# Late fetch of weights, fillers on TensorE, and half the pauses between row scatters in a hybrid layer kernel

## What is computed

```python
x = x + attn_a(_layernorm(x), Wq, Wk, Wv, Wo, bo, q_norm_w, k_norm_w)
x = x + ffn(_layernorm(x), gate_weight, Wg, Wu, Wd, Sg, Su, Sd)
x = x + attn_b(_layernorm(x), Wa, Wx, ba, bx, Lam)
x = x + ffn(_layernorm(x), gate_weight, Wg, Wu, Wd, Sg, Su, Sd)
```

## Time and profile before

| | |
|---|---|
| median of 3 runs | 1233.53 us (1233.43 to 1235.91) |
| the profiled execution | 1236.23 us, its span 1234.1 us |
| busy in the span | PE 997.5 us (81%), ACT 739.3 (60%), DVE 520.1 (42%), POOL 410.5 (33%) |
| mean granted clock of TensorE | 0.90 of 2.4 GHz |
| chain that ended last | PE 29% of the span, POOL 11%, issue 4%, DMA 3%, DVE 3% |

### The profile page before, as it was taken

How to read it: one execution, slowest core, us unless ns; L and a number is a source line. 1 busy time by engine, 2 the same in 40 slices (tenths; PEclk the granted TensorE clock), 3 DMA queues, 4 the chain that set the end, 5 groups by cost and what they waited for, 6 DMA issues and landing times.

```text
span 1234.1 us, 20310 instructions
## 1 busy us (share of the span) xinstructions
PE 997.5 (81%) x7268; PEld 644.7 (52%) x7268; DVE 520.1 (42%) x1575; ACT 739.3 (60%) x982; POOL 410.5 (33%) x404
## 2 busy tenths in 40 slices
PE   5888777886898788977638999944887774999978
PEld 3543232331345446444328999922454434999966
DVE  7772711454212333521332333348875741333325
ACT  3588899999999999999103444414453400444430
POOL 0000000000230025055143556610388884566550
PEclk9999888989998999999678999956888976999987
DMA  9992000000110002000498999548132524999948
GB/s 352 394 392 78 1 1 1 18 2 11 49 50 23 18 33 90 2 21 4 142 264 234 292 289 290 109 151 271 50 121 109 160 66 125 268 290 279 268 63 330
DMA packets 94948, 176.21 MB, mean 143 GB/s; under 512 B 13134, under 2 KB 46895, under 8 KB 94848
## 3 DMA queue, kind: packets, MB, share of 16 engines
q1 hardware_dynamic: 57744, 129.86, 31.5%
q0 software_dynamic: 23616, 28.44, 10.9%
q10 hardware_dynamic: 13488, 16.62, 4.9%
HBM read 107.30 MB, written 83.72 MB: 155 GB/s over the span
## 4 chain that ended last, share of the span: by engine, by line
PE 29%; POOL 11%; issue 4%; DMA 3%; DVE 3%; DVEq 1%; ACT 0%; POOLq 0%; SPq 0%; ACTq 0%
PE PS L1459 14%; PE PS L1470 9%; POOL expert_in L335 8%; POOL pause L343 3%; PE PS L1446 2%; PE PS L1515 1%; DMA XE<-expert_in 1%; PE PS L1499 1%; DMA spare_space<-expert_out 1%; DMA expert_in<-xp,didx 1%; PE PS L1548 1%; DMA expert_out<-ob,yidx 1%; PE PS L1389 0%; PE PS L1404 0%; POOL expert_out L1345 0%
## 5 line engine op out<-in xcount | busy, mean ns | idle before, releaser
L335 POOL DMA_INDIRECT expert_in<-xp,didx x192 | 193.6, 1008 | 618.2 <-ACT PR L779 496.6
L774 ACT ACTIVATE PR<-PS 128x1024 f32<-128x1024 f32 (+3 forms) x312 | 276.5, 960 | 30.8 <-PE PS L643 15.2
L779 ACT ACTIVATE PR<-PR 128x2048 f32<-128x2048 f32 (+3 forms) x156 | 274.1, 1759 | 0.0
L1345 POOL DMA_INDIRECT expert_out<-ob,yidx x128 | 180.6, 1411 | 157.4 <-ACT ob L1657 117.5
L663 PE MATMUL PS<-PR,V 128*32 128x512 f32 (+3 forms) x768 | 94.9, 568 | 43.4 <-ACT PR L779 43.4
L1906 DVE SCALAR_TENSOR_TENSOR gta<-gth,PS 88x192 f32<-88x192 f32 x128 | 44.8, 350 | 192.8 <-ACT gth L1647 192.8
L643 PE MATMUL PS<-QT,KT 96*128 96x512 bf16 (+3 forms) x384 | 103.7, 363 | 12.4 <-ACT PR L774 9.8
L1647 ACT ACTIVATE gth<-PS 88x192 f32<-88x192 f32 x128 | 41.8, 326 | 106.6 <-PE PS L1459 106.6
L1657 ACT ACTIVATE ob<-PS,wslot 96x256 f32<-96x256 f32 x128 | 60.1, 469 | 62.1 <-PE PS L1470 59.9
L1459 PEld LDWEIGHTS PS<-XT,spare_space 128*88 128x88 f32 x960 | 91.7, 163 | 8.8 <-issue 2.6
L668 PE MATMUL PS<-PR,V 128*32 128x256 f32 x960 | 66.8, 392 | 34.9 <-ACT PR L779 34.6
(11 more groups left out here) (271 smaller groups left out, 1552.6 us busy)
## 6 DMA issues: line engine op xcount, KB each, us to landing
spare_space<-in_wgu SPq DMA_DIRECT2D x60, 352.0 KB
expert_out<-zero SPq DMA_DIRECT2D x2, 8256.0 KB, 50.5
expert_in<-zero SPq DMA_DIRECT2D x2, 7776.0 KB, 39.4
XE<-expert_in ACTq DMA_DIRECT2D x32, 486.0 KB
WGU<-in_wgu SPq DMA_DIRECT2D x44, 352.0 KB
spare_space<-expert_out SPq DMA_DIRECT2D x24, 512.0 KB, 6.2
spare_space<-in_wd SPq DMA_DIRECT2D x60, 176.0 KB
shared_space<-in_wgu SPq DMA_DIRECT2D x24, 352.0 KB
```

Of the source, the lines that this page charges most:

```text
L335: pool.indirect_dma_start(out=buf_d[f], out_offset=bass.IndirectOffsetOnAxis(ap=didx[b][:, r, j:j + 1], axis=0), in_=xp[b][:, r, :], in_of ...
L774: act.activation(PR[:, n % 3, 2 * pr:2 * pr + 2, cols(v, s):CW], PS[:, S0 + 2 * pr:S0 + 2 * pr + 2, cols(v, s):CW], ACT.Tanh, scale=1.0 / ...
L779: act.activation(PR[:, n % 3, :, lo:CW], PR[:, n % 3, :, lo:CW], ACT.Exp, scale=SOFT_CAP).then_inc(exp_done, 1)
L1345: pool.indirect_dma_start(out=y_d[f], out_offset=bass.IndirectOffsetOnAxis(ap=yidx[:, n % 4, j:j + 1], axis=0), in_=ob[:, i % EU, :], in_o ...
```

## The change

On GpSimd the pause follows every second row scatter instead of each. On SP the weights of experts 10 to 13 and wab are issued after the first XE has landed, wab behind them. On TensorE `fill(n)` issues n matmuls of 128x256 whose result, in bank 7, nobody reads; it stands at eleven places around the expert passes and between them, and in combine_late the wait on out_copied moves ahead of the one on O95, with 15 fillers between them. Before the fillers that follow the first pass a wait on out_copied is added.

```diff
-                    if pause is not None:
-                        n = CT * TOPK * (k - NC) + r * TOPK + j
+                    if pause is not None and j % 2:
+                        n = (CT * TOPK * (k - NC) + r * TOPK + j) // 2
                         if n:
                             pool.wait_ge(paused, n)
                         pool.memset(pause[:], 0.0).then_inc(paused, 1)
...
             first_spare(0)
+            sp.wait_ge(x_ld[0], 16)
+            first_spare2(0)
             sp.dma_start(wab[:], wab_d).then_inc(wab_loaded, 16)
-            first_spare2(0)
             experts(0)
...
+            def fill(n, bank=V0):
+                for _ in range(n):
+                    pe.matmul(PS[:, bank, 0:2 * P], const("ident"), consts[:, 0:2 * P], start=True, stop=True, skip_group_check=True)
...
             def combine_late():
                 pe.wait_ge(xt_ready, NH * 2)
+                pe.wait_ge(out_copied, 2 * E)
+                fill(15)
                 pe.wait_ge(o95_loaded, 32)
-                pe.wait_ge(out_copied, 2 * E)
...
             shared_down(K0)
+            fill(14)
             experts(0)
+            pe.wait_ge(out_copied, E)
+            fill(12)
             overflow_rows(0)
+            fill(4)
             overflow_rows(1)
+            fill(13)
             turn_recur(0)
             for c in range(NC + 1):
                 k = NC + c - 1
                 if c:
+                    fill(8 if c == 1 else 2)
                     turn_rows(k)
                     logits(k)
                 if c < NC:
                     gates(c)
+                if c == 0:
+                    fill(12)
                 if c:
                     place(k)
...
                 if c < NC:
+                    fill(8 if c == 0 else 2)
                     turn_state(c)
...
             shared_down(NC + K0)
+            fill(14)
             experts(1)
             combine_late()
```

## The result

The changed kernel takes 1220.36 us in the median (1218.26 to 1224.97), the kernel before on the same chip 1234.72 (1233.43 to 1236.26): a ratio of 0.9892, with a 95% interval of 0.9861 to 0.9922. The profiled execution took 1218.63 us, its span 1216.4. The prediction was 1215.5, between 1206 and 1226. On one of the chips that the experiments used, the very same kernel was not faster at all (1.0022). That is the second result of this study. The experiments show where the time goes there, and leave open which path inside the chip is held up.

A forecast was written before the change was run, and what follows sets the result against it. Passes are TensorE-bound; gains lie around them, in XE's wait, VectorE's and GpSimd's routing, and the end. 6.0 + 0 + 8.3 + 2.7 + 1.0 = 18.0 less than 1236.23 gives 1218.2; 2.7 lower for the median, 1215.5; range 1206 to 1226.

The forecast's parts named there:

- Part 1: In front of the first pass: weights issued behind XE let it load in 4.18 instead of 10.40 us; 6.0 us won.
- the rival's 3.7: In front of the first pass: older weights have a tail, so 3.7 us won; with a cold second start 1221, chance 0.17.
- The rule of the Trainium skill: DMA engines alternate between queues packet by packet; by turns alone XE takes 5.2 us, making the sum 1.0 us smaller.
- Part 2 and 3: Filler price 0.48 us warm, 0.93 cold; fillers around the first pass and in routing, 0 before the pass, 0.9 at turn_state.
- The slower rival: Fillers behind gates(0) run cold and delay the overflow matmuls; 9.1 us slower, 1243 us, chance 0.06.
- Part 4: Middle-stage scatters: 36 pauses fewer, then routing takes over the chain from GpSimd; 8.3 us won, bounds 5.5 and 11.3.
- denser scatters hold other engines: Rival in the middle-stage scatters: VectorE's small operations wait for scatter pairs, so 6.7 us lost there; 1230.5 us, chance 0.05.
- Part 5: Second expert pass: 14 fillers leave a 0.9 us gap before XE, so it starts warm; 2.7 us won, cold 0.
- shared_down ends at 1025.65 less 1.8: Before the second pass: step placing the 14 fillers at 1023.9 to 1030.6, with XE at 1031.5.
- Part 6: The end: 15 fillers speed the overflow matmuls, VectorE then sets the end; 1.0 us taken, between 1.7 won and 0.6 later.
- The likeliest case: The whole kernel: the forecaster's own case, 1210 to 1220 us, chance 0.55.
- the rival with a tail and a cold start: Older weights slow XE before the first pass and the second pass starts cold; 1221 us, chance 0.17.

The follow-up runs named there:

- ring_late: Changed kernel with the weights of experts 14 to 21 also issued behind the first XE: 1235.27 us, ratio 0.9996, on the chip where the unchanged changed kernel took 1237.03.
- fill_only: Kernel before with the fillers alone and their two waits on out_copied: 1232.68 us, ratio 1.0001.
- pause_only: Kernel before with half the pauses alone: 1223.36 us, ratio 0.9918.
- no_fill: Changed kernel with fillers of length zero, leaving late fetch and half pauses: 1223.63 us, ratio 0.9908.
- late_only: Kernel before with the late fetch alone: 1230.34 us, ratio 0.9979.
- after_again: The changed kernel, unchanged, measured again on another chip against the kernel before: 1237.03 us, ratio 1.0022.
- long_fill: Changed kernel with 32 and 28 fillers in place of 14 before the first and second expert pass: 1238.61 us, ratio 1.0042.
- the first comparison: The study's main measurement, the changed kernel against the kernel before on the same chip: 1220.36 against 1234.72 us, ratio 0.9892.
- pair_pause: Changed kernel with a second, short memset and its wait behind the pause after every second scatter: 1239.36 us, ratio 1.0049.
- three_quarters: Changed kernel with a pause left out behind every fourth scatter only: 1226.38 us, ratio 0.9942.
- no_pause: Changed kernel with no pauses at all between scatters: 1274.71 us, ratio 1.0306.

## Why the prediction was right in its number, and where not

**Part 1, the late fetch: the mechanism right, the size wrong.** I took 6.0 "because the volume says so" and 3.6 us were found. The mis-sized term is the end of the older weights: reckoned from the mean rate of the stretch they were through at 638, and ring_late shows that they are what still slows XE (6.47 with them, 4.44 without) and the last scatter (6.30 and 1.92, on the same chip). The row that spoke for a tail, wab's 16.9 us, was the better witness: the rival's 3.7 is next to what was measured. The rule of the Trainium skill that I had weighed against the step (DMA: Bandwidth & Descriptors, "Queues, rings and completion order": the engines take turns between queues) made it 5.2 us for XE with the new weights gone; measured are 6.00 to 8.55. The trace agrees with the rule in that a queue of weights slows XE without blocking it. Neither the rule nor my volume counted the older weights.

No clear wait of the pass on the late weights came up: 155.34 us, and 154.9 to 156.2 in the eight other first passes that have this late fetch and began cold, against 155.1 to 155.4 in the three without it. The pass has room for four late experts, and ring_late shows that it has none for twelve.

**Part 2 and 3, fillers.** Prices (0.44 us each warm, where I had 0.48) and covers hold. The 12 behind gates(0) ran warm, 5.34 us for 24 records, and the overflow matmuls behind them ended at 838.52, half a microsecond before VectorE's addition at 839.08, which came without a wait. The slower rival, cold fillers at this place, didn't occur. The transposes took 1.09 us, and VectorE's wait behind them fell as reckoned. After:

```profile
844.21 1.09 PE L1563 MATMUL PS<-consts,spare_space 128*128 128x128 f32 x8 [2.04 <-DVE spare_space L2020]
...
845.34 1.22 DVE L2028 TENSOR_TENSOR X<-X,PS 128x1024 f32<-128x1024 f32 x1 [0.93 <-PE PS L1563]
```

In the profile before the same addition waited 1.80 us. Of these 0.9 us, 0.5 are left at the first scatter. fill_only at 1.0001 says what that is worth in the whole: less than can be measured.

**Part 4, the pauses: right, with its hand-over.** 8.5 us were found up to the last scatter, the earlier start included, where 8.3 were predicted, and routing took over by waits for the row numbers. They stand before the second and the third chunk, where I had named the third and the last. pause_only and no_fill repeat the length within 0.3 us. The kernel before is not the same in every execution either: with all pauses the scatters took 149.23 us in late_only and 149.59 in fill_only, not 150.39, so 7 to 8 us are the pauses'. What failed here is the weight of a rival: that denser scatters hold other engines got 0.05 and 1230.5 us. It is real, and on the chip of after_again it took back more than this part's whole gain (12.7 us). I had set against it that the unpaused scatters of 618 to 634 do nothing of the kind. That is right for the profile I had, and the unpaused last chunk of 31 us would have said the same. It was wrong to take it for every chip: on the chip of after_again this very stretch is held up, from 11 us behind its first scatter on. I had also looked at VectorE's small operations only, with the rule on the port pair that VectorE and GpSimd share (the Trainium skill, SBUF — State Buffer, "Terms": held for a whole instruction while the other waits). A single row fits it, L248 with 0.72 us instead of 0.25. Nearly all of the time is lost otherwise: durations stay, distances grow, and ACT and TensorE are held as well, which that rule doesn't give.

**Part 5, the warm second pass: wrong in its condition.** A warm start is worth about what I said: the second pass took 154.2 us in the five profiles in which it began warm and 156.7 to 157.5 in the nine others, and long_fill won 2.8 in the first. But in the first comparison there was none. In the profile after:

```profile
1009.33 6.21 PE L1486 MATMUL PS<-consts 128*128 128x256 f32 x28
1022.84 1.51 PE L1447 MATMUL PS<-consts,XE 96*128 96x96 f32 x8 [7.31 <-DMA XE<-expert_in]
```

The step that failed is "shared_down ends at 1025.65 less 1.8". Counted from the first scatter it ended after 136.0 us, not after 142.6. This end isn't steady: 136.2 in late_only, 139.1 in fill_only, 139.7 in pair_pause. So the fillers were through early, and the gap became 7.3 us instead of 0.9. Neither the fillers nor the clock explains it: late_only, pause_only and no_fill have no fillers and end after 135.7 to 136.2 us at clocks of 0.87 and 0.88, and fill_only, at 0.89, after 139.1. It is the 142.6 of the one profile that I had which stands apart, and why stays open. In after_again the unpaused scatters of the last chunk held the fillers up as well, and the second pass took 154.17 us: it did begin warm, but 9.2 us after the last scatter instead of 7.0, so 2.2 of the 3.1 us are gone again. A fixed number of fillers meets a gap whose length depends on what happens 100 us earlier.

**Part 6, the end: not decided.** 1.1 us were found where 1.0 was predicted, but the stretch from the last pass to the end was 35.0 to 37.5 us in ten profiles with these fillers and 34.6 to 37.8 in four without. No effect of the fillers can be read from that. What I had expected to see, VectorE ending the program, is there.

**The sum.** The likeliest case as I had told it (late fetch at 6.0 and a warm second pass) didn't occur. What the trace shows is the rival with a tail and a cold start, 1221 us, and 1220.36 were measured. The forecast of 1215.5 lies 4.9 us off: 2.4 of Part 1 and 2.7 of Part 5 are missing, and Part 4, the largest term, was right. That the first comparison fell on a chip where nothing is held up is luck: on the chip of after_again the same prediction would have met 1237.03 us and a ratio of 1.0022, outside its range.

**What stays open.** Which path is held up is not shown, nor what sets a held chip apart. Whether it is semaphores or instructions on their way is a guess either way that no run tests; the instruction queues carried the same number of packets in both profiles of the changed kernel (60 and 41). It isn't shown either whether it is the chip or the hour, since each chip was used once; that all profiles of one chip are of one kind, four on the chip of after_again and seven on two others, speaks for the chip. The kernel with all its pauses was never profiled on a held chip: that they keep the middle stage free there rests on its times alone, 1233.77 and 1233.44 us against 1233.01 and 1233.57 on the others.

**The version to keep.** On an undisturbed chip half pauses with late fetch (0.9892, 0.9908, 0.9912) are the best of those run, not told apart from half pauses alone (0.9918), and the fillers can go. Fewer pauses still were not tried there. Where every chip counts, the late fetch with all pauses (0.9979, itself not run on a held chip) is the safe part by what is known, and three_quarters (0.9942) the candidate to measure on more chips.

## What to carry to other kernels

A pause between GpSimd's indirect DMAs that looks like lost time can, on some chips, be what keeps the other engines running: before it is thinned out, profile the kernel on more than one chip and look, wherever scatters already come without a pause, at the distances between tiny operations of the other engines, not at their durations. In this case fillers paid only where the gap behind them was short (0.95 us, not 7.3); measure the gap again after every other change, and in more than one execution. A backlog in a DMA queue is better judged by the landing time of its last member than by bytes over mean rate.

## What the runs showed of the hardware that was not expected

- On two of the chips, indirect DMAs issued 1.28 us apart hold up TensorE, ScalarE and VectorE alike: an operation of 0.17 us came every 1.4 us instead of every 0.24, for as long as the scatters went on (in no_pause from 15 to 31 us behind the first). At 1.43 us in the mean 12.7 us were lost there over three chunks. In the nine profiles of the other chips nothing is held up at 1.28, 1.43 or 1.57 us apart. At 1.57 on the first two no profile was taken.
- It doesn't depend on the bytes: 68 values a row gave 54.18 us a chunk, 324 values 55.14.
- The 0.10 us memset of one column, with a wait for the memset before it, lengthened a pair of scatters by 0.63 us.
